# The softmax of a local-attention stage, rewritten as one ScalarE exponential per head and tile that reads the scores in PSUM

## What is computed

```python
for i in range(DEPTH):                                  # 6 layers
    x = attn_layer(shift_tokens(x), ...) + x
    x = ffn_layer(shift_tokens(x), ...) + x

def attn_layer(x, Wqkv, qs, ksc, Wo):                   # 16 heads of 64
    q, k, v = split(x @ Wqkv)
    q, k = l2norm(q) * qs, l2norm(k) * ksc
    q = q * cos * scale + rotate_half(q) * sin * scale
    k = k * cos * inv + rotate_half(k) * sin * inv      # inv = 1 / scale
    out = local_attention(q, k, v)                      # windows of 32, each looks at 64 keys
    return out @ Wo

sim  = einsum('bhwie,bhwje->bhwij', bq, bk2) * 8.0
attn = softmax(where(mask, -max, sim), -1)
out  = einsum('bhwij,bhwje->bhwie', attn, bv2)
```

## Time and profile before

| | us |
|---|---|
| median of 3 runs | 1990.13 (1988.86 to 1998.07) |
| the profiled execution: its time | 1990.29 |
| the profiled execution: its span | 1988.5 |
| first and last start of the instruction that makes `rinv`, one for each step | 54.3 and 1860.1 |

### The profile page before, as it was taken

One profiled execution on the slowest core, in us unless ns is written; L12 is line 12 of the kernel. 1 busy time (PEld: TensorE's weight loads), 2 busy tenths in 40 slices (PEclk: granted clock), 3 DMA queues, 4 the chain that ended last, 5 costly groups with the idle time before them and its releaser, 6 DMA issues. The chain is left out here.

```text
span 1988.5 us, 73877 instructions
## 1 busy us (share of the span) xinstructions
PE 1774.7 (89%) x30944; PEld 1004.7 (51%) x30944; DVE 1704.8 (86%) x2592; ACT 1262.0 (63%) x2355; POOL 1633.2 (82%) x1350
## 2 busy tenths in 40 slices
PE   3899999999989999999999999999989899999872
PEld 1455555555545554555555555555545555555520
DVE  5789998989987899889889889888998799998636
ACT  3567757667676576667676675765766676766630
POOL 2778998978988799879898899887998789987851
PEclk9899999999999999999999999999999999999975
DMA  3123432242323423134231523234241443214221
GB/s 101 34 42 56 80 58 53 55 74 38 63 50 78 66 37 61 43 58 83 57 58 31 80 57 58 65 59 63 37 75 34 85 73 54 38 29 74 47 32 42
DMA packets 95606, 113.13 MB, mean 57 GB/s; under 512 B 42334, under 2 KB 61548, under 8 KB 95276
## 3 DMA queue, kind: packets, MB, share of 16 engines
q1 hardware_dynamic: 95276, 108.41, 30.3%
HBM read 19.22 MB, written 1.05 MB: 10 GB/s over the span
## 5 line engine op out<-in xcount | busy, mean ns | idle before, releaser
L1313 POOL TENSOR_TENSOR AB<-qc,qn 128x512 f32<-128x512 f32 x384 | 521.9, 1365 | 25.1 <-DVE qn L1107 24.8
L1324 POOL TENSOR_TENSOR AB<-AB,rinv 128x512 f32<-128x512 f32 x384 | 442.9, 1168 | 43.3 <-DVE rinv L1130 43.3
L544 PE MATMUL bank<-wqkv,XT 128*128 128x512 f32 x768 | 420.6, 631 | 8.4 <-DVE qn L1107 4.9
L824 ACT ACTIVATE sq<-bank 128x512 f32<-128x512 f32 x384 | 227.9, 594 | 160.9 <-PE bank L544 156.4
L1331 POOL TENSOR_TENSOR Pb<-Pb,p_rden 128x512 f32<-128x512 f32 x192 | 211.4, 1101 | 128.7 <-DVE p_rden L1151 127.6
L833 ACT ACTIVATE qkT<-bank 128x512 f32<-128x512 f32 x384 | 229.9, 599 | 100.5 <-PE bank L569 98.1
L1114 DVE TENSOR_REDUCE ssq<-sq 128x8 f32<-128x512 f32 x384 | 255.4, 666 | 37.2 <-ACT sq L824 37.1
L1107 DVE TENSOR_TENSOR qc<-bank,rt 128x512 f32<-128x512 f32 x384 | 258.9, 674 | 32.0 <-ACT sq L824 26.4
L569 PEld LDWEIGHTS bank<-ident,AB 128*128 128x128 f32 x1536 | 175.4, 142 | 196.5 <-issue 103.6
L1107 DVE TENSOR_TENSOR qn<-bank,rt 128x512 f32<-128x512 f32 x384 | 260.6, 679 | 0.0
L618 PEld LDWEIGHTS bank<-PT,V 64*64 64x64 f32 x12288 | 199.7, 136 | 112.8 <-issue 80.5
(11 more groups left out here) (133 smaller groups left out, 2788.1 us busy)
## 6 DMA issues: line engine op xcount, KB each, us to landing
V<-V SPq DMA_DIRECT2D x672, 64.0 KB
rep<-du SPq DMA_DIRECT2D x64, 512.0 KB, 7.5
wqkv<-in_Wqkv SPq DMA_DIRECT2D x36, 256.0 KB, 3.7
XV<-XT SPq DMA_DIRECT2D x96, 64.0 KB, 2.8
wo<-in_Wo SPq DMA_DIRECT2D x6, 512.0 KB
BC<-BC SPq DMA_DIRECT2D x8, 256.0 KB
w<-in_W SPq DMA_DIRECT2D x6, 341.0 KB, 5.7
BC<-BC SPq DMA_DIRECT2D x8, 128.0 KB
```

Of the source, the lines that this page charges most:

```text
L544: pe.matmul(R[u % 2][:], XT[:, s % NB, (u % 2) * P:(u % 2 + 1) * P], wqkv[:, (u // 2) * 512:(u // 2 + 1) * 512], start=True, stop=True).th ...
L824: act.activation(sq[:, u % 2, :], R[u % 2][:], ACT.Square).then_inc(sq_done, 1)
L1313: pool.tensor_tensor(AB[:, n % NAB, :], qc[:, u % 2, :], qn[:, u % 2, :], ALU.add).then_inc(rs_done, 1)
L1324: pool.tensor_tensor(o, o, r, ALU.mult).then_inc(nm_done, 1)
```

## The change

The exponential is computed straight from the scores in PSUM by ACT, with a per-row scale and a per-row bias, and the row sum comes out of the same instruction's accumulator. A scale per row is a scale per head and tile, so a group takes 8 instructions of 64 elements where it took one of 512. Since the scale can carry the query's normaliser, queries are no longer normalised ahead of the transposes: `normalise` works on the keys alone (256 elements a unit). DVE loses the subtraction and the row sum; it keeps the maximum and gets `nb`, minus the maximum times the normaliser, and once a step `rq`, the normaliser with sign and factor. The factor 8 of the scores moves into the keys' rotary table (-4 / scale, against the -2 in `rinv`). `scores` and `values_out` now wait for `exp_done` where they waited for `sub_done`. All six order lists are written anew, the loop begins one iteration earlier (for `arrange_x(i + 2)`), and the Mamba block's `z_dbc`, `z_dup` and what follows them start two or three iterations later than before relative to its input.

```diff
-FIRST_TO_LAST = range(-1, STEPS + 9)
+FIRST_TO_LAST = range(-2, STEPS + 9)
...
-X_ORDER = [("values_out", 3, 1, 1), ("scores", 0, 0, 1), ("scores", 1, 0, 1), ("values_out", 0, 0, 1),
-           ("scores", 2, 0, 1), ("values_out", 1, 0, 1), ("scores", 3, 0, 1), ("values_out", 2, 0, 1)]
+X_ORDER = [("values_out", 2, 1, 1), ("values_out", 3, 1, 1), ("scores", 0, 0, 1), ("scores", 1, 0, 1),
+           ("values_out", 0, 0, 1), ("values_out", 1, 0, 1), ("scores", 2, 0, 1), ("scores", 3, 0, 1)]
...
-                    pe.wait_ge(sub_done if kind == "scores" else OT_done, 4 * s + n + 1)
+                    pe.wait_ge(exp_done if kind == "scores" else OT_done, 4 * s + n + 1)
...
             def expo(s, g):
...
-                act.wait_ge(sub_done, 4 * s + g + 1)
-                act.activation(Pb[:, g % 2], Pb[:, g % 2], ACT.Exp, scale=QK_SCALE / 4.0).then_inc(exp_done, 1)
+                n = 4 * s + g
+                act.wait_ge(mx_done, n + 1)
+                if n >= 2:
+                    act.wait_ge(pt_full, n - 1)
+                    act.wait_ge(den_done, n - 1)
+                for odd in range(2):
+                    for c in range(2):
+                        for tl in range(TILES):
+                            e = 4 * odd + 2 * c + tl
+                            col = 16 * g + e
+                            j = (2 * c + tl) * 2 * WIN
+                            ins = act.activation(Pb[:, g % 2, e, :], SB[:, odd, j:j + 2 * WIN], ACT.Exp,
+                                                 scale=rq[:, s % 2, col:col + 1], bias=nb[:, g % 2, e:e + 1],
+                                                 accum_out=den[:, g % 2, e:e + 1])
+                ins.then_inc(exp_done, 1)
...
+                dve.wait_ge(rinv_done, s + 1)
+                if s >= 2:
+                    dve.wait_ge(exp_done, 4 * (s - 1))
+                dve.tensor_scalar(rq[:, s % 2, :], rinv[:], -0.5, None, ALU.mult).then_inc(rq_done, 1)
...
-            def softmax(s, g):
...
-                dve.tensor_tensor(Pb[:, g % 2].rearrange("p (o h) j -> p o h j", o=2), src,
-                                  mx[:].rearrange("p (o h e) -> p o h e", o=2, e=1).broadcast_to([P, 2, 4, 2 * WIN]),
-                                  ALU.subtract).then_inc(sub_done, 1)
...
+            def row_max(s, g):
...
+                link(dve.reduce_max(mx[:].rearrange("p (o h) -> p o h", o=2), SB.rearrange("p o (h j) -> p o h j", h=4), AX_X))
+                dve.wait_ge(rq_done, s + 1)
...
+                dve.scalar_tensor_tensor(nb[:, g % 2], mx[:], -1.0, rq[:, s % 2, 16 * g:16 * g + 8], ALU.mult, ALU.mult)\
+                   .then_inc(mx_done, 1)
...
-                link(dve.reduce_sum(den[:, g % 2, :], Pb[:, g % 2], AX_X))
                 dve.reciprocal(rden[:, g % 2, :], den[:, g % 2, :]).then_inc(den_done, 1)
...
             def normalise(s, u):
...
-                o = AB[:, (8 * s + u) % NAB, :].rearrange("p (h d) -> p h d", d=DH)
-                r = rinv[:, 8 * u:8 * u + 8].rearrange("p (h o) -> p h o", o=1).broadcast_to([P, 8, DH])
+                o = AB[:, (8 * s + u) % NAB, 256:512].rearrange("p (c o d) -> p c o d", c=2, d=DH)
+                r = heads(rinv[:, 16 * (u // 2):16 * (u // 2) + 16], u % 2)[:, 1]
+                r = r.rearrange("p c (o e) -> p c o e", e=1).broadcast_to([P, 2, 2, DH])
```

More of the change, by code:

```diff
@@ L747, in _ @@
             for i in FIRST_TO_LAST:
+                values_out(i - 1, 2)
+                z_x(i + 1)
+                z_g(i - 4)
+                turn_p(i - 1, 3)
+                z_dbc(i - 2)
+                var_x(i - 3)
+                value(i, 2)
+                turn(i, 0)
                 values_out(i - 1, 3)
-                turn(i, 0)
-                value(i, 1)
+                value(i, 3)
                 turn(i, 1)
-                value(i, 2)
+                qk(i + 1, 0)
+                scores(i, 0)
@@ L753, in _ @@
                 turn(i, 2)
-                scores(i, 0)
+                z_dup(i - 3)
                 z_sum(i - 7, 4)
-                value(i, 3)
-                qk(i + 1, 0)
+                z_sum(i - 5, 1)
+                w_out(i - 2, 0)
                 turn(i, 3)
-                w_out(i - 2, 0)
-                w_gelu(i - 3, 0)
                 qk(i + 1, 1)
+                qk(i + 1, 2)
                 scores(i, 1)
                 turn_p(i, 0)
-                qk(i + 1, 2)
                 w_out(i - 2, 1)
-                z_sum(i - 5, 1)
+                w_gelu(i - 3, 0)
@@ L767, in _ @@
+                z_sum(i - 5, 2)
                 turn(i, 4)
[L768 to L769 removed]
+                qk(i + 1, 3)
+                qk(i + 1, 4)
+                turn(i, 5)
                 values_out(i, 0)
[L771 to L772 removed]
                 w_gelu(i - 3, 1)
[L774 to L777, removed]
                 turn_p(i, 1)
                 qk(i + 1, 5)
[L780 removed]
@@ L794, in _ @@
-                values_out(i, 2)
+                z_out(i - 9)
+                w_out(i - 2, 2)
+                w_out(i - 2, 3)
+                qk(i + 1, 7)
+                z_sum(i - 7, 5)
+                w_gate(i - 3, 2)
+                scores(i, 3)
+                w_down(i - 3)
                 z_sum(i - 6, 3)
                 z_sum(i - 8, 6)
-                w_down(i - 3)
                 z_sum(i - 4, 0)
                 z_sum(i - 8, 7)
-                z_dup(i)
-                z_g(i - 4)
@@ L1409, in _ @@
                 normalise(i, 2)
+                z_hc(i - 6, 6)
+                normalise(i, 3)
+                normalise(i, 4)
+                z_bu(i - 4, 0)
+                z_bu(i - 4, 1)
+                z_bu(i - 4, 2)
+                z_hc(i - 5, 4)
+                z_hc(i - 5, 5)
                 z_bu(i - 7, 11)
-                z_bu(i - 6, 8)
-                z_hc(i - 7, 9)
-                rotate_sum(i, 6)
-                normalise(i, 3)
+                normalise(i, 5)
+                rotate_sum(i, 7)
@@ L1430, in _ @@
                 z_hc(i - 8, 12)
+                z_hc(i - 7, 9)
+                normalise(i, 6)
+                normalise_p(i, 0)
+                rotate_sum(i + 1, 0)
+                z_hc(i - 4, 0)
+                z_hc(i - 7, 10)
+                z_bu(i - 5, 7)
+                z_hc(i - 8, 13)
+                rotate_sum(i + 1, 1)
+                z_bu(i - 7, 12)
                 normalise_p(i, 1)
-                z_hc(i - 8, 13)
+                z_bu(i - 7, 13)
+                rotate_sum(i + 1, 2)
@@ L1559, in constants @@
     tab = np.zeros((P, 2, TILES, 2, DH), f)
-    for c, sc in enumerate((scale, (f(1.0) / scale).astype(f))):
+    for c, sc in enumerate((scale, (f(-4.0) / scale).astype(f))):
         for z, tr in enumerate((cos, sin)):
```

301 lines of the change are left out of this document (142 added, 159 removed).

## The result

The changed kernel takes 2096.2 us (median, 2086.6 to 2104.6) against 1989.9 before: 1.053 times the time, 95% interval 1.049 to 1.057. Slower was forecast, with 2040 us and a range of 1950 to 2185; the loss is 106 us where 50 was forecast, so the size is off by a factor of two.

The account below looks back on a forecast made before the run. PE was taken as the bound, 35.86 of 38.4 us a step. PE's way gave 39.3 us and ACT's 38.7; 39.4 was taken, +47 us over 47 steps plus 3 for the tail: 2040 us, range 1950 to 2185.

Parts of the forecast that it names:

- The relief for PE: With POOL less busy, PE's wait for POOL's scaling of the probabilities should mostly go: a gain of 1.3 us a step.
- The hold of the banks: Score banks stay held from the maximum until the last exponential: 4.6 us per group instead of 1.4 us.
- the price of an exponential: On ACT, one 64-element exponential with its accumulator output: 0.43 us start to start, ends 0.33 and 0.63.
- PE's way: Step time seen from PE: 35.9 us work, 2.25 stalls and 1.2 other idle time, together 39.3 us.
- bank stalls: PE waiting for held score banks: 1.2 us in even and 3.3 in odd iterations, 2.25 us on average.
- today's idle time that is not POOL's: PE's present idle time apart from waiting for POOL, carried over unchanged: 1.2 us a step.
- start and tail: Outside the steps: the start gains nothing, the tail's longer chain for one group adds 3 us.
- copies in front of the exponentials: In ACT's queue: the prediction is wrong if copies make the eight exponentials start late; no size given.
- Rival 2: ACT becomes the plain bound at 0.53 us an exponential: 2160 us, 2240 at 0.63 us; chance 0.30.
- Rival 1: On ACT the accumulator costs nothing, 0.33 us an exponential (deciding under about 0.38): 1965 us, or 1930 without stalls; chance 0.26.
- the bank chain: Per group: maximum 0.68, `nb` 0.20, semaphores about 0.1, seven starts of 0.43, a last 0.43 plus 0.1; given as 4.6 us.
- the chances: Whole kernel's time against before: faster 0.25, same 0.12, slower 0.63.

Follow-up runs that it names:

- old_one_exp: Changed kernel with one constant-scale 512-element exponential per group, no accumulator, on the order lists and loop start of the kernel before: 0.967, 1931 us.
- one_exp: Changed kernel, new lists kept, with one 512-element exponential per group, constant scale and bias, no accumulator: 1.011, 2017 us.
- no_read: Changed kernel with its eight exponentials per group but without the accumulator output, row sums replaced by a constant: 1.013, 2021 us.
- old_order: Changed kernel's softmax with the six order lists and loop start of the kernel before: 1.222, 2439 us.
- busy_first: one_exp with eight short idle ACTIVATEs in front of each group's exponential, so the banks are held longer: 1.041, 2077 us.
- busy_spread: one_exp with 32 idle ACTIVATEs a step, one behind each copy, square and exponential: 1.017, 2023 us.
- scale_no_max: Kernel before, own lists, queries not normalised by POOL; DVE multiplies scores by the query normaliser instead of subtracting, no maximum taken: 0.956, 1906 us.
- busy_after: one_exp with eight short idle ACTIVATEs behind each group's exponential, after the banks are released: 1.040, 2073 us.

## Why the prediction was half right

**The ledger.** In parts of the 1990 us, each from two rows of the table: POOL's and DVE's relief, with one exponential that frees the banks (old_one_exp): 0.967 - 1 = -65 us. The new lists (one_exp less old_one_exp): 1.011 - 0.967 = +88. Eight exponentials for one (no_read less one_exp): +3. The reads (changed kernel less no_read): 1.053 - 1.013 = +80. Sum +106. The terms come from different chips and each has an interval of about 0.5%. They also hang on the order in which they are taken, because list and block work on each other: with the block put on the old lists first (old_order less old_one_exp) it costs 507 us, and the new lists then give back 336.

**Right.** DVE 29.7 forecast, 29.34 measured; `normalise` 0.77 us by the straight line, 0.78 measured; POOL 30.4 against 29.47. The relief for PE, 1.3 us x 47 = 61 us, against 65 to 71. That ACT's block would hurt, and the sign. The hold of the banks as well: at 0.38 us an exponential the prediction's working gives 4.15 us, and the trace has 4.3 in the median; the exponentials start 0.2 us after `nb` on average, so ACT was ready for them.

**Mis-sized, the price of an exponential.** 0.43 us was taken, 0.38 measured, between the rival's 0.33 and the forecast. ACT's work is 35.0 us a step, not 37.3. The prediction said that below about 0.38 the change would pay. Put 0.38 into its own working: the banks are held 4.15 us, PE stalls 0.75 and 2.1 us in even and odd iterations, 1.4 on average, a step takes 38.5 us and the kernel about 1998. The sum with the right price is 98 us short. Its 2040 was nearer only because one error covered part of another.

**The step that failed.** "PE's way: 35.9 of work, 2.25 of bank stalls, and 1.2 of today's idle time that is not POOL's". It took today's other idle time as it stood and added stalls against the new list, as though the new lists brought nothing else. The step of one_exp, which has no long block to stall for, tests this term alone: 35.9 + 1.2 = 37.1 us by the prediction's working, 37.1 measured on the old lists (old_one_exp), 38.8 on the new ones. Over 47 steps that is 83 of the 88 us (with the old softmax in them the new lists cost even more, 155 us). The prediction used them as a source of gaps and never asked what they give up for these gaps. A small rest of the miss is start and tail: 10 us where 3 were counted.

**The mechanism inside it.** The stalls were laid to the held banks. That their size, 2.25 us a step, is near the 40.65 - 38.83 = 1.8 us that block and reads cost on the new lists is partly luck, since the price was 1.4 at the right 0.38 us and the place was another. The runs put most of the stalls elsewhere: a block of 3 us in ACT's queue costs the same whether the banks wait for it or not, and the profile after has PE waiting 32.1 us for copies against 24.5 for exponentials. The prediction named this as what could prove it wrong, the other way about (copies in front of the exponentials), and gave it no price. busy_first stays 1.2% below the changed kernel. Its block is 0.1 us shorter (3.09 against 3.20 us from first start to last end, in the medians), which beyond the threshold can be a part of that; the rest stays open.

**The rivals.** Rival 2 gave 2160 us for ACT as plain bound; ACT is busy 86% of the step, and busy_spread shows that its total costs nearly nothing, so it didn't happen. Rival 1 would not have come out with its own price either: no_read runs at 0.29 us an exponential, below the 0.33 of that rival, and is still 1.3% slower than before, with the new lists at fault.

**Small slips.** The terms of the bank chain add up to 4.5 us, not 4.6, and the chances to 0.13 for the same and 0.62 for slower; neither moves the forecast by more than 8 us.

**Open.** Which moves in the six lists cost the 88 us. PE's busy time rose from 35.86 to 36.66 us a step with the same instructions. It isn't that the matmuls of a group took more time: the groups' busy times, each taken by itself, add up to 2040 us before and 2034 after, at the same mean granted clock of 0.958, so neighbouring groups overlap less. Why they do wasn't tested. How much of the lists' price goes through the clock is open too. And whether lists made for the softmax of scale_no_max would beat 1906 us wasn't tried.

## What to carry to other kernels

An order list and the operations in it are one design: price a rewritten list by itself, by running the old work in it, since here it cost as much (88 us) as the block it was made for (83 us). On an in-order engine that serves many short requests, count the longest unbroken block besides the total, because 32 extra operations a step were nearly free one by one and cost 3% in blocks of 3 us. How long a block may be is read off the list: it is the work that the waiting engine has between its request and its next need of the answer (here two `qk`). Before splitting an operation into eight to carry a factor, look for an engine that already passes over the data: here the multiplication took the subtraction's place on VectorE, the bound of 8 on the scores made the maximum needless, and the relief came without the block.

## What was not expected of the hardware

Short ACTIVATEs with scale and bias from SBUF start 0.29 us apart in both cases seen here, 16 elements ((2.43 - 0.39) / 7, the idle ones of busy_after) or 64 ((2.47 - 0.45) / 7, no_read). The two differ in function and source as well (Identity from SBUF, Exp from PSUM), so this shows no more than that the 48 extra elements don't appear in the spacing.

```profile
917.80 2.43 ACT L857 ACTIVATE stage<-ident,eps 128x16 f32<-128x16 f32 x8
```

The Trainium skill ("ScalarE: Activation LUTs", "What ACT_TABLE_LOAD costs") gives 186 ns and 0.833 ns an element, 93 ns for each pointer operand, less 93 ns of overlap: an estimate of 0.33 us for 64 elements. The row's length agrees (413 ns against 425), the spacing of 0.29 us doesn't, and the measurement decides. By these rows the overlap is 0.41 - 0.29 = 0.12 us. For the 16 elements the same working gives an estimate of 0.29 us, which is what was measured. An accumulator read lasts 0.215 us and adds 0.09 us from one exponential to the next.
